# The D term of a selective scan added by a diagonal matrix, its sums read out by ScalarE, and one step-size operation moved from GpSimd to VectorE

## The chip, the core and the metric

The kernel runs on one core of a Trainium2 chip. The metric is the device time of one execution in microseconds, here the median of three runs.

## What is computed

The input x has 8 sequences (batches below) of 1024 steps and 256 channels. A block modulates x, runs a selective scan (Mamba) over each sequence, adds the result, modulates again, and adds a mixture of eight experts, of which each token takes two. Cut to what matters here:

```python
h = _layernorm(x) * (1 + ca) + sa
x_dbl = einsum('bld,ed->ble', h, W_x)              # dt_raw (64), B_sel (16), C_sel (16)
dt = softplus(einsum('blr,dr->bld', dt_raw, W_dt) + b_dt)
A_bar = exp(dt[..., None] * -exp(A_log))
dB_u = (dt * h)[..., None] * B_sel[:, :, None, :]
h_state = scan over l of  A_bar * previous + dB_u
y = einsum('bldn,bln->bld', h_state, C_sel)
x = x + ga * (y + h * D_param)
h2 = _layernorm(x) * (1 + cb) + sb
x = x + gb * mixture_of_experts(h2)
```

The modulation vectors sa, ca, ga, sb, cb, gb come from a small matmul at the start; ga and D_param are inputs, one number for each channel (ga also for each batch).

## The kernel before

**Work and its pieces.** Channels lie on partitions, the 1024 steps along the free dimension. A batch has 32 units: two halves of 128 channels (hf), four groups of states (q), four groups of channels (j). A unit is one tile of 128 partitions (32 channels by 4 states) by 1024. For each unit, ScalarE makes exp(A dt) (`decay`, line 624, into one of three buffers av), VectorE multiplies the spread B in PSUM by dt*u (`times_b`, line 821, the product by B) and scans (`scan`, line 828, into one of eight buffers h), and GpSimd multiplies by C (`times_c`, line 955). For each four units TensorE spreads the next B over the partitions (`spread_b`, line 466, one pair of banks, so it waits for the last product of the four before) and sums the products over the states with a mask that also holds ga (`sums`, line 485, called y). Four such groups make one half of a batch in the banks Y.

**The residual.** When the four groups of a half are summed, VectorE's step zs (line 847) makes ga*D*hT + sums and writes it over hT, in one instruction of 128x1024; TensorE transposes it (`residual`, line 561), and VectorE adds x (zX, line 857).

**The step size.** With v the matmul of dt_raw plus the bias, softplus is relu(v) + log(1 + exp(-|v|)), and for small exp(-|v|) a correction is added: with e = exp(-|v|) and up = 1 + e as rounded, it is log(up) - ((up - 1) - e). ScalarE makes |v|, relu, e, up and the logarithm (lines 658 to 670; tiles sp_t and src), VectorE's step corr makes (up - 1) - e (line 841), and GpSimd's step dt has three operations of 128x512: log minus the correction (line 964), plus relu, which is dt (line 966), and dt times u (line 969). The matmul of dt (line 519), those for B and C (line 514), and the reads of C share one bank. SyncE then copies dt and dt*u, each from 32 partitions to four places, to dd (lines 400 and 407), from which ScalarE and VectorE take them.

**The experts.** GpSimd multiplies h2T by the gates, for two experts at a time (xg, line 987, one of two buffers), TensorE multiplies by the weights (`expert`, line 581: 8 matmuls for each xg, 16 records in the trace, since each fp32 matmul shows as two) and adds the bias (line 589), ScalarE scales (line 704), TensorE transposes (line 550), VectorE adds to x (line 862). There are 16 xg for each batch, and they run beside the units of the next batch. Those of the last batch come behind the last scan.

**What sets the order.** Each engine executes its own list in order. The lists come from one table of times, AT, in units from the start of a batch: `schedule` gives each step a time and sorts, and each engine takes its steps from the sorted list. No step carries out of order, and a wait holds up all that is behind it on its engine. Waits are on counting semaphores: `s_y` counts the groups of sums, `s_z` the residual halves, `s_lp` GpSimd's first step-size operation; `release` and `emptied` are for the shared banks.

```python
            put(s + AT["corr"], "corr", b, hf, c)
            put(s + AT["dt"], "dt", b, hf, c)
...
        put(t + 16 * hf + 16 + AT["zs"], "zs", b, hf)
...
    return [step for _, step in sorted(at, key=lambda p: p[0])]
```

Of the kernel before, what the change touches and what calls it, by code (L numbers as in the profile page):

```python
# [24 lines left out]
AT = dict(exp=0.53, mul=0.02, scan=0.93, ch=8.04, Bs=0.64, y=7.8, stat0=-3.57, stat0s=0.69, rstd0=1.5,  # L25
          rsb0=0.03, xh0=3.5, xh0s=0.29, xT0=15.38, xT0h=0.55, xTs=3.16, rxT0=-0.28, wx=4.64, rwx=-0.1,
          S=-1.08, ldx=34.2, gam=18.44, dl0=20.23, dl1=36.04, dls=3.41, rdl=0.34, corr=0.46, dt=7.7, C=26.08,
          CS=2.58, Cc=1.19, rC=0.34, ddt=37.03, ddts=1.6, ddu=37.35, ddus=2.04, zs=4.0, ldx2=35.93, z=4.84,
          zX=-0.7, zd=2.37, stat1=6.15, stat1s=0.46, rstd1=10.38, rsb1=0.48, xh1=11.48, xh1s=0.0, xh1g=1.96,
          xT1=11.74, xT1h=0.15, xT1s=1.42, rxT1=0.53, lg=13.82, rlg=0.76, lT=0.16, soft=0.58, softe=0.3,  # L30
          top=0.97, gT=1.37, rgT=-0.42, gw=11.16, gr=32.81, xg=23.11, xgs=1.78, gl=-1.9, f=-3.08, fE=0.89,
          o=3.02, oX=1.85, out=11.61, md1=-34.75, gates=-33.15, ga=-25.15, bn0=-118.76, bn0s=9.06,
          stat1A=4.38, stat1B=9.56, stat1sA=4.37, stat1sB=20.83, rstd1A=2.83, rstd1B=8.42, rsb1A=3.19,
          rsb1B=1.49, xh1A=7.29, xh1B=26.22, xh1sA=0.0, xh1sB=0.0, xh1gA=22.13, xh1gB=3.45, xT1A=7.43,
          xT1B=24.5, xT1hA=0.0, xT1hB=1.19, xT1sA=3.31, xT1sB=12.26, rxT1A=2.4, rxT1B=4.65, lgA=9.1,
          lgB=69.91, rlgA=1.11, rlgB=-7.93, lTA=1.32, lTB=5.57, softA=1.74, softB=-9.93, softeA=0.39,
          softeB=4.13, topA=5.19, topB=2.3, gTA=2.65, gTB=16.94, rgTA=-0.31, rgTB=1.96, gwA=20.35, gwB=6.85,
          grA=57.71, grB=94.08, xgA=38.5, xgB=129.13, xgsA=4.99, xgsB=8.34, glA=8.49, glB=20.82, fA=21.21,
          fB=-7.62, fEA=76.63, fEB=43.38, oA=35.72, oB=68.53, oXA=17.7, oXB=61.07, outA=58.55, outB=89.32,
          stat1P=6.67, stat1sP=0.31, rstd1P=9.57, rsb1P=0.13, xh1P=10.69, xh1sP=0.0, xh1gP=2.8, xT1P=12.61,  # L40
          xT1hP=0.0, xT1sP=0.58, rxT1P=0.47, lgP=14.2, rlgP=-0.07, lTP=0.1, softP=0.18, softeP=0.3, topP=0.5,
          gTP=0.86, rgTP=0.23, gwP=10.31, grP=30.17, xgP=22.53, xgsP=1.69, glP=-2.42, fP=-3.58, fEP=0.38,
          oP=4.43, oXP=9.99, outP=34.06)
# [978 lines left out]
```

## Time and profile before

| what | value |
|---|---|
| median of 3 runs | 1219.75 us (1219.33 to 1220.39) |
| the profiled execution, its own time | 1223.0 us |
| its span in the trace | 1221.1 us |
| granted TensorE clock over the span | 0.875 of full |
| VectorE busy | 1024.6 us, 84% |
| GpSimd busy | 1025.0 us, 84% |
| TensorE busy (matmuls) | 943.9 us, 77% |
| ScalarE busy | 712.3 us, 58% |

The profile is of one execution. Its engines are named PE (TensorE), PEld (its weight loads), DVE (VectorE), ACT (ScalarE), POOL (GpSimd) and SP (SyncE, which only issues DMAs; SPq is its queue of instructions). L828 is line 828 of the kernel. A share of busy time is a mean over the whole span, in which the start (the first scan begins at 49.56 us) and the end behind the last scan have other limits than the middle, so stretches and single rows are needed to tell which engine the others wait for.

### The profile page before, as it was taken

What the parts mean: (1) busy time and instruction counts of PE and PEld (TensorE: products, weight loads), DVE (VectorE), ACT (ScalarE), POOL (GpSimd) and SP (SyncE); (2) the same over time, 40 slices, a digit from 0 to 9 for tenths busy, and PEclk for the clock granted to TensorE, in tenths of its full rate; (3) what the DMA queues carried; (4) which work ended last, traced back from release to release, by engine and by line L of the source; (5) the groups of instructions that cost most, each with busy time, mean ns of one, the idle gap of its engine ahead of it and who ended that gap; (6) DMA issues with size and microseconds to landing.
All of it is one profiled execution on the core that took longest, in us unless ns stands there. A gap on an engine that the chain in (4) does not pass through costs nothing. (4 is left out here: it accounts for less than half of the span.)

```text
span 1221.1 us, 13597 instructions
## 1 busy us (share of the span) xinstructions
PE 943.9 (77%) x4235; PEld 591.0 (48%) x4235; DVE 1024.6 (84%) x826; ACT 712.3 (58%) x1412; POOL 1025.0 (84%) x512
## 2 busy tenths in 40 slices
PE   6234543588978888788977888788978986889998
PEld 4101111245644555455554555455644664557787
DVE  2399999999899989999999989999999999995110
ACT  4764578456775579547856678457855366331200
POOL 1477766699999999899999999899989999798453
PEclk9556655589998889899999989999998999889899
DMA  5607060536425371637244551637152533521221
GB/s 163 160 14 181 27 137 1 119 84 171 114 68 146 105 185 44 150 86 193 74 104 106 155 146 46 165 96 183 42 138 81 154 106 94 124 70 52 82 77 61
DMA packets 90552, 131.21 MB, mean 107 GB/s; under 512 B 13536, under 2 KB 73512, under 8 KB 90480
## 3 DMA queue, kind: packets, MB, share of 16 engines
q1 hardware_dynamic: 90480, 130.34, 41.2%
q8 instruction: 34, 0.56, 0.2%
q14 instruction: 38, 0.31, 0.1%
HBM read 54.50 MB, written 8.65 MB: 52 GB/s over the span
## 5 line engine op out<-in xcount | busy, mean ns | idle before, releaser
L955 POOL TENSOR_TENSOR h<-h,Cr 128x1024 f32<-128x1024 f32 x256 | 603.0, 2375 | 64.0 <-DVE h L828 62.2
L828 DVE TENSOR_TENSOR_SCAN h<-av,ps 128x1024 f32<-128x1024 f32 x256 | 584.8, 2284 | 18.0 <-ACT av L624 1.6
L581 PE MATMUL ps<-xg,we 128*128 128x256 f32 x2048 | 495.6, 398 | 30.6 <-POOL xg L987 26.9
L581 PEld LDWEIGHTS ps<-xg,we 128*128 128x128 f32 x2048 | 399.2, 199 | 127.5 <-POOL xg L987 39.5
L987 POOL TENSOR_TENSOR xg<-h2T,gbc 128x1024 f32<-128x1024 f32 x128 | 304.1, 2378 | 62.8 <-DMA gbc<-gates 31.7
L821 DVE TENSOR_TENSOR ps<-ps,dd 128x1024 f32<-128x1024 f32 x256 | 315.4, 1232 | 45.4 <-DMA dd<-src 16.1
L624 ACT ACTIVATE av<-dd,An 128x1024 f32<-128x1024 f32 x256 | 288.2, 1141 | 52.4 <-DVE h L828 40.8
L485 PE MATMUL ps<-h,gam 128*32 128x512 f32 x1024 | 161.7, 761 | 15.4 <-POOL h L955 9.4
L466 PE MATMUL ps<-S,sel 64*128 64x512 f32 x128 | 52.4, 492 | 56.8 <-DVE ps L821 56.5
L704 ACT ACTIVATE z<-ps,md 128x256 f32<-128x256 f32 x64 | 26.7, 468 | 97.9 <-PE ps L589 75.5
L485 PEld LDWEIGHTS ps<-h,gam 128*32 128x32 f32 x1024 | 32.1, 128 | 97.9 <-issue 84.1
L678 ACT ACTIVATE Cr<-ps 128x512 f32<-128x512 f32 x64 | 37.7, 591 | 63.0 <-PE ps L526 42.6
L519 PE MATMUL ps<-rows,wrow 64*128 64x512 f32 x64 | 44.4, 781 | 32.7 <-DVE S L835 24.4
L862 DVE TENSOR_TENSOR X<-ps,X 128x512 f32<-128x512 f32 x32 | 21.9, 684 | 54.3 <-PE ps L550 54.3
L466 PEld LDWEIGHTS ps<-S,sel 64*128 64x128 f32 x128 | 21.7, 210 | 94.4 <-DVE ps L821 80.5
L658 ACT ACTIVATE sp_t<-ps,bd 128x512 f32<-128x512 f32 x32 | 21.8, 683 | 65.9 <-PE ps L519 65.9
L526 PE MATMUL ps<-S,sel 64*128 64x512 f32 x64 | 33.8, 531 | 30.9 <-ACT Cr L678 28.4
L505 PE MATMUL ps<-identf,sp_t 128*128 128x128 f32 x128 | 23.5, 317 | 31.4 <-ACT sp_t L735 20.1
L976 POOL TENSOR_TENSOR gam<-mask,ga 128x256 f32<-128x256 f32 x8 | 5.1, 631 | 48.0 <-DMA ga<-md 27.2
L964 POOL TENSOR_TENSOR src<-src,sp_t 128x512 f32<-128x512 f32 x32 | 41.4, 1294 | 3.5 <-DVE sp_t L841 3.5
L969 POOL TENSOR_TENSOR src<-src,hT 128x512 f32<-128x512 f32 x32 | 40.8, 1274 | 2.5
L966 POOL TENSOR_TENSOR src<-src 128x512 f32<-128x512 f32 x32 | 40.7, 1271 | 2.5
(100 smaller groups left out, 830.6 us busy)
## 6 DMA issues: line engine op xcount, KB each, us to landing
dd<-src SPq DMA_DIRECT2D x512, 128.0 KB, 2.5
gbc<-gates SPq DMA_DIRECT2D x128, 256.0 KB, 3.6
X<-in_x SPq DMA_DIRECT2D x8, 1024.0 KB, 7.3
out<-X SPq DMA_DIRECT2D x32, 256.0 KB, 2.3
XN<-in_x SPq DMA_DIRECT2D x7, 1024.0 KB, 7.1
we<-in_We SPq DMA_DIRECT2D x2, 1024.0 KB, 9.1
XN<-in_x SPq DMA_DIRECT2D x2, 512.0 KB, 4.7
Cr<-in_wmod SPq DMA_DIRECT2D x1, 1024.0 KB, 5.7
```

The source lines that it names most:

```text
L466: e = pe.matmul(ps[:, BQ + c], sel[R:P, q], S[R:P, b % 2, c * CH:(c + 1) * CH], start=True, stop=True)
L485: e = pe.matmul(ps[32 * j:32 * j + 32, Y + c], gam[:, b % 2, 2 * j + hf], h[:, (4 * g + j) % HS, c * CH:(c + 1) * CH], start=(q == 0), sto ...
L519: e = pe.matmul(bk, wdt[:, hf * P:(hf + 1) * P], dtr[:, c * CH:(c + 1) * CH], start=True, stop=True)
L581: e = pe.matmul(bk[:, m * 256:(m + 1) * 256], we[:, hf, 2 * ep + e2, m * P:(m + 1) * P], xg[:, i % XG, e2, hf], start=(ep == e2 == m == hf ...
L624: act.activation(av[:, u % AS], dd[:, j, 0], ACT.Exp, scale=An[:, 0, i:i + 1]).then_inc(s_a, 1)
L821: dve.tensor_tensor(wide(BP), wide(BQ), dd[:, j, 1], ALU.mult).then_inc(s_bm, 1)
L828: dve.tensor_tensor_scan(h[:, u % HS], av[:, u % AS], wide(BP), 0.0, ALU.mult, ALU.add).then_inc(s_scan, 1)
L955: pool.tensor_tensor(h[:, u % HS], h[:, u % HS], Cr[:, q], ALU.mult).then_inc(s_ch, 1)
L964: pool.tensor_tensor(src[:, 1, cs], src[:, 1, cs], sp_t[:, 1], ALU.subtract).then_inc(s_lp, 1)
L966: pool.tensor_tensor(src[:, 0, cs], src[:, 1, cs], src[:, 0, cs], ALU.add).then_inc(s_dt, 1)
L969: pool.tensor_tensor(src[:, 1, cs], src[:, 0, cs], hT[:, b % 2, hf, cs], ALU.mult).then_inc(s_dtu, 1)
L987: pool.tensor_tensor(xg[:, i % XG], h2T[:, :, 256 * c:256 * c + 256].unsqueeze(1).to_broadcast([P, 2, 2, 256]), gbc[:, i % GL].unsqueeze(2 ...
```

## The change

1. VectorE's step zs goes. A diagonal matrix dg (128x128 for each half, the identity scaled by ga*D, made by ScalarE in the new step dg) is multiplied with hT on TensorE, eight matmuls of 32x512 ahead of the first group of sums of each half, in the same accumulation. ScalarE then copies the finished sums from the two banks Y to hT (the new zs).
2. In the step size, VectorE's corr becomes two operations: log + e into the bank, then (up - 1) minus that, over the logarithm in src. GpSimd subtracts the result from relu, which is dt; its step has two operations in place of three. ScalarE's wait for `s_lp` ahead of up becomes a wait for VectorE's release of the bank.
3. The table AT has other numbers.

```diff
+    put(t + AT["dg"], "dg", b)
...
+                if q == 0:
+                    pe.wait_ge(s_dg, b + 1)
                 for c in range(2):
+                    if q == 0:
+                        for j in range(NJ):
+                            pe.matmul(ps[32 * j:32 * j + 32, Y + c], dg[:, hf, 32 * j:32 * j + 32],
+                                      hT[:, b % 2, hf, c * CH:(c + 1) * CH], start=True, stop=False)
                     for j in range(NJ):
                         e = pe.matmul(ps[32 * j:32 * j + 32, Y + c], gam[:, b % 2, 2 * j + hf],
-                                      h[:, (4 * g + j) % HS, c * CH:(c + 1) * CH], start=(q == 0), stop=(q == NQ - 1))
+                                      h[:, (4 * g + j) % HS, c * CH:(c + 1) * CH], start=False, stop=(q == NQ - 1))
...
                     if i:
-                        act.wait_ge(s_lp, i)
+                        emptied(act, ("dl", i // 4 - (i % 4 == 0), (i - 1) % 4 // 2, (i - 1) % 2))
...
+                elif s[0] == "dg":
+                    b = s[1]
+                    if b == 0:
+                        act.wait_ge(s_md, 2)
+                    if b:
+                        act.wait_ge(s_y, 8 * b - 3)
+                    for hf in range(2):
+                        e = act.activation(dg[:, hf], identf[:], ACT.Copy, scale=Dga[:, hf, b:b + 1])
+                    e.then_inc(s_dg, 1)
+                elif s[0] == "zs":
+                    _, b, hf = s
+                    act.wait_ge(s_y, 8 * b + 4 * hf + 4)
+                    act.activation(hT[:, b % 2, hf], wide(Y), ACT.Copy).then_inc(s_z, 1)
...
                     use = ("dl", b, hf, c)
-                    release(dve.scalar_tensor_tensor(out=sp_t[:, 1], in0=sp_t[:, 1], scalar=-1.0, in1=mb(use), op0=ALU.add,
+                    l = src[:, 1, c * CH:(c + 1) * CH]
+                    link(dve.tensor_tensor(mb(use), mb(use), l, ALU.add))
+                    release(dve.scalar_tensor_tensor(out=l, in0=sp_t[:, 1], scalar=-1.0, in1=mb(use), op0=ALU.add,
                                                      op1=ALU.subtract), use)
-                elif s[0] == "zs":
-                    _, b, hf = s
-                    dve.wait_ge(s_y, 8 * b + 4 * hf + 4)
-                    z = hT[:, b % 2, hf]
-                    dve.scalar_tensor_tensor(out=z, in0=z, scalar=Dga[:, hf, b:b + 1], in1=wide(Y), op0=ALU.mult,
-                                             op1=ALU.add).then_inc(s_z, 1)
...
                     emptied(pool, ("dl", b, hf, c))
-                    pool.tensor_tensor(src[:, 1, cs], src[:, 1, cs], sp_t[:, 1], ALU.subtract).then_inc(s_lp, 1)
-                    pool.wait_ge(s_lp, i + 1)
-                    pool.tensor_tensor(src[:, 0, cs], src[:, 1, cs], src[:, 0, cs], ALU.add).then_inc(s_dt, 1)
+                    pool.tensor_tensor(src[:, 0, cs], src[:, 0, cs], src[:, 1, cs], ALU.subtract).then_inc(s_dt, 1)
```

**The order on VectorE, fifth batch, from unit 19 on.** S<-ps,S is the low part of C's rows of the next batch. In the kernel before, L821 is the product by B, L828 the scan, L835 S, L847 zs, L841 corr:

```order
L821 TENSOR_TENSOR ps<-ps,dd 128x1024
L828 SCALAR_TENSOR_TENSOR h<-av,ps 128x1024
L847 SCALAR_TENSOR_TENSOR hT<-hT,Dga,ps 128x1024
L821 TENSOR_TENSOR ps<-ps,dd 128x1024
L841 SCALAR_TENSOR_TENSOR sp_t<-sp_t,ps 128x512
L828 SCALAR_TENSOR_TENSOR h<-av,ps 128x1024
L821 TENSOR_TENSOR ps<-ps,dd 128x1024
L828 SCALAR_TENSOR_TENSOR h<-av,ps 128x1024
L821 TENSOR_TENSOR ps<-ps,dd 128x1024
L835 TENSOR_TENSOR S<-ps,S 32x512
```

The same place in the changed kernel, where L842 is the product, L849 the scan, L856 S, and L863 with L864 corr:

```order
L842 TENSOR_TENSOR ps<-ps,dd 128x1024
L849 SCALAR_TENSOR_TENSOR h<-av,ps 128x1024
L842 TENSOR_TENSOR ps<-ps,dd 128x1024
L863 TENSOR_TENSOR ps<-ps,src 128x512
L864 SCALAR_TENSOR_TENSOR src<-sp_t,ps 128x512
L849 SCALAR_TENSOR_TENSOR h<-av,ps 128x1024
L842 TENSOR_TENSOR ps<-ps,dd 128x1024
L856 TENSOR_TENSOR S<-ps,S 32x512
```

zs is gone, corr has two instructions, and S stands one unit earlier. Elsewhere in a batch corr of the first columns of the second half moves from behind product 4 to behind scan 3 of the next batch's units.

**The order on TensorE at the same place**, from one spread of B to the next. In the kernel before, L581 is an expert group, L514 the matmul for B and C, L519 the matmul of dt, L485 y, L466 the spread of B:

```order
L581 MATMUL ps<-xg,we 128x256 x8
L514 MATMUL ps<-hT,wx 128x512 x2
L581 MATMUL ps<-xg,we 128x256 x8
L519 MATMUL ps<-rows,wrow 128x512
L485 MATMUL ps<-h,gam 32x512 x8
L466 MATMUL ps<-S,sel 128x512 x2
```

In the changed kernel (L490 the diagonal matmuls, L493 y, L468 the spread):

```order
L589 MATMUL ps<-xg,we 128x256 x8
L522 MATMUL ps<-hT,wx 128x512 x2
L589 MATMUL ps<-xg,we 128x256 x8
L527 MATMUL ps<-rows,wrow 128x512
L490 MATMUL ps<-hT,dg 32x512 x4
L493 MATMUL ps<-h,gam 32x512 x4
L490 MATMUL ps<-hT,dg 32x512 x4
L493 MATMUL ps<-h,gam 32x512 x4
L468 MATMUL ps<-S,sel 128x512 x2
```

The list is the same but for the diagonal matmuls, which stand ahead of the spread. The group of y with them has twice the matmuls.

**The end of GpSimd's list**, in the kernel before (L955 the product by C, L987 xg):

```order
L987 TENSOR_TENSOR xg<-h2T,gbc 128x1024
L955 TENSOR_TENSOR h<-h,Cr 128x1024
L987 TENSOR_TENSOR xg<-h2T,gbc 128x1024
L955 TENSOR_TENSOR h<-h,Cr 128x1024 x2
L987 TENSOR_TENSOR xg<-h2T,gbc 128x1024 x22
```

and in the changed one (L972 the product by C, L1002 xg):

```order
L1002 TENSOR_TENSOR xg<-h2T,gbc 128x1024
L972 TENSOR_TENSOR h<-h,Cr 128x1024 x2
L1002 TENSOR_TENSOR xg<-h2T,gbc 128x1024
L972 TENSOR_TENSOR h<-h,Cr 128x1024 x2
L1002 TENSOR_TENSOR xg<-h2T,gbc 128x1024 x23
```

One xg more stands behind the last product by C.

## Rows read from the trace of the kernel before

**Rows 1.** Stretches: length, busy time and instructions of each engine, TensorE's clock, DMA
```profile
core 0: us, PE busy (x) PEld busy (x) DVE busy (x) ACT busy (x) POOL busy (x), PEclk, DMA share, GB/s
69.00:184.00 115.00, 56.10 (x182) 16.40 (x182) 110.64 (x68) 66.06 (x113) 86.74 (x44) 0.63 0.38 92
654.00:772.00 118.00, 100.90 (x464) 65.35 (x463) 110.69 (x80) 80.96 (x171) 113.92 (x56) 0.94 0.42 111
```

**Rows 2.** VectorE in order of time, fifth batch, units 18 to 21 (start us, length us)
```profile
659.22 2.29 DVE L828 TENSOR_TENSOR_SCAN h<-av,ps 128x1024 f32<-128x1024 f32 x1
661.42 1.26 DVE L847 SCALAR_TENSOR_TENSOR hT<-hT,Dga,ps 128x1024 f32<-128x1024 f32 x1
662.59 1.23 DVE L821 TENSOR_TENSOR ps<-ps,dd 128x1024 f32<-128x1024 f32 x1
663.73 0.68 DVE L841 SCALAR_TENSOR_TENSOR sp_t<-sp_t,ps 128x512 f32<-128x512 f32 x1
664.32 2.28 DVE L828 TENSOR_TENSOR_SCAN h<-av,ps 128x1024 f32<-128x1024 f32 x1
666.64 1.23 DVE L821 TENSOR_TENSOR ps<-ps,dd 128x1024 f32<-128x1024 f32 x1
667.96 2.29 DVE L828 TENSOR_TENSOR_SCAN h<-av,ps 128x1024 f32<-128x1024 f32 x1
```

**Rows 3.** Order of time at the start, GpSimd and VectorE
```profile
35.01 1.26 POOL L964 TENSOR_TENSOR src<-src,sp_t 128x512 f32<-128x512 f32 x1
36.35 1.26 POOL L966 TENSOR_TENSOR src<-src 128x512 f32<-128x512 f32 x1
...
40.26 1.27 POOL L966 TENSOR_TENSOR src<-src 128x512 f32<-128x512 f32 x1
...
48.29 1.23 DVE L821 TENSOR_TENSOR ps<-ps,dd 128x1024 f32<-128x1024 f32 x1 [10.11 <-DMA dd<-src]
```

**Rows 4.** Order of time at the end: last scan, last products by C, last experts
```profile
1107.34 2.29 DVE L828 TENSOR_TENSOR_SCAN h<-av,ps 128x1024 f32<-128x1024 f32 x1
...
1109.74 4.71 POOL L955 TENSOR_TENSOR h<-h,Cr 128x1024 f32<-128x1024 f32 x2
...
1200.30 14.08 PE L581 MATMUL ps<-xg,we 128*128 128x256 f32 x64
```

**Rows 5.** Groups by line: busy us, mean ns of one, idle time before and its releasers
```profile
L847 DVE SCALAR_TENSOR_TENSOR hT<-hT,Dga,ps 128x1024 f32<-128x1024 f32 x16 | 20.1, 1257 | 6.3 <-PE ps L485 6.3
L964 POOL TENSOR_TENSOR src<-src,sp_t 128x512 f32<-128x512 f32 x32 | 41.4, 1294 | 3.5 <-DVE sp_t L841 3.5
L485 PE MATMUL ps<-h,gam 128*32 128x512 f32 x1024 | 161.7, 761 | 15.4 <-POOL h L955 9.4
L678 ACT ACTIVATE Cr<-ps 128x512 f32<-128x512 f32 x64 | 37.7, 591 | 63.0 <-PE ps L526 42.6
```

**Rows 6.** VectorE's waits (total, times, longest), then single rows about the waits for spreads
```profile
DVE ps L821 <- PE ps L466: 16.0, 11, 4.2
...
704.10 3.72 PE L581 MATMUL ps<-xg,we 128*128 128x256 f32 x16 [0.28 <-POOL xg L987]
...
709.62 1.23 DVE L821 TENSOR_TENSOR ps<-ps,dd 128x1024 f32<-128x1024 f32 x1 [1.32 <-PE ps L466]
...
718.96 0.69 DVE L862 TENSOR_TENSOR X<-ps,X 128x512 f32<-128x512 f32 x1 [0.68 <-PE ps L550]
...
725.47 1.25 DVE L847 SCALAR_TENSOR_TENSOR hT<-hT,Dga,ps 128x1024 f32<-128x1024 f32 x1
...
726.75 0.59 ACT L670 ACTIVATE src<-ps 128x512 f32<-128x512 f32 x1
...
728.57 1.23 DVE L821 TENSOR_TENSOR ps<-ps,dd 128x1024 f32<-128x1024 f32 x1 [1.85 <-PE ps L466]
...
674.01 2.90 PE L485 MATMUL ps<-h,gam 128*32 128x512 f32 x16
676.84 0.73 PE L466 MATMUL ps<-S,sel 64*128 64x512 f32 x2
678.31 1.23 DVE L821 TENSOR_TENSOR ps<-ps,dd 128x1024 f32<-128x1024 f32 x1
```

More of the change, by code:

```diff
@@ L20 @@
 BP, BQ, Y, FB, MB = 0, 2, 4, 6, 7
[L25 to L43, printed above, removed]
@@ new lines @@
+AT = dict(exp=0.59, mul=0.43, scan=0.96, ch=7.78, Bs=0.44, y=7.6, stat0=-4.54, stat0s=0.89, rstd0=2.74,
+          rsb0=0.6, xh0=4.31, xh0s=0.27, xT0=15.23, xT0h=0.42, xTs=2.79, rxT0=0.56, wx=4.56, rwx=-0.56,
+          S=-0.62, ldx=32.82, gam=24.87, dg=39.13, dl0=20.18, dl1=35.75, dls=3.34, rdl=0.63, corr=0.47,
+          dt=7.55, C=26.12, CS=2.5, Cc=0.92, rC=0.35, ddt=37.04, ddts=2.42, ddu=37.96, ddus=2.38, zs=4.38,
+          ldx2=45.74, z=5.23, zX=-0.54, zd=2.16, stat1=6.33, stat1s=0.53, rstd1=10.61, rsb1=0.09, xh1=10.92,
+          xh1s=0.19, xh1g=1.06, xT1=12.22, xT1h=0.0, xT1s=1.4, rxT1=0.08, lg=13.63, rlg=0.08, lT=0.4,
+          soft=0.94, softe=-0.22, top=1.06, gT=1.34, rgT=0.42, gw=10.17, gr=32.45, xg=23.0, xgs=1.78,
+          gl=-1.86, f=-3.08, fE=1.03, o=2.8, oX=2.34, out=20.48, md1=-19.28, gates=-24.81, ga=-20.38,
+          bn0=-78.02, bn0s=5.5, stat1A=6.02, stat1B=7.93, stat1sA=19.78, stat1sB=30.22, rstd1A=4.66,
+          rstd1B=16.88, rsb1A=4.34, rsb1B=0.0, xh1A=9.01, xh1B=17.46, xh1sA=0.07, xh1sB=2.33, xh1gA=27.4,
+          xh1gB=2.12, xT1A=8.51, xT1B=39.47, xT1hA=0.1, xT1hB=4.62, xT1sA=2.21, xT1sB=15.61, rxT1A=3.27,
+          rxT1B=2.43, lgA=10.46, lgB=76.49, rlgA=2.49, rlgB=-20.32, lTA=1.01, lTB=17.54, softA=1.37,
+          softB=41.67, softeA=1.66, softeB=-10.5, topA=15.02, topB=46.43, gTA=3.65, gTB=39.11, rgTA=1.9,
+          rgTB=9.48, gwA=13.83, gwB=67.25, grA=103.18, grB=175.9, xgA=52.72, xgB=186.07, xgsA=13.74,
+          xgsB=26.38, glA=17.37, glB=11.13, fA=17.19, fB=6.58, fEA=49.37, fEB=28.42, oA=57.91, oB=37.69,
+          oXA=34.38, oXB=63.52, outA=97.14, outB=66.98, stat1P=7.31, stat1sP=0.21, rstd1P=9.63, rsb1P=0.54,
+          xh1P=10.69, xh1sP=0.07, xh1gP=0.82, xT1P=11.33, xT1hP=0.22, xT1sP=0.97, rxT1P=0.14, lgP=12.75,
+          rlgP=1.03, lTP=0.02, softP=0.81, softeP=0.65, topP=0.83, gTP=0.64, rgTP=2.1, gwP=11.81, grP=32.49,
+          xgP=21.34, xgsP=1.95, glP=-4.1, fP=-3.17, fEP=2.41, oP=3.48, oXP=11.77, outP=35.08)
@@ L270, in adaln_block @@
         bns, bna = sb("bns", [P, 4, 6]), sb("bna", [P, BLK, 2])
+        dg = sb("dg", [P, 2, P])
         pe_t, G = sb("pe_t", [P, BLK, E]), sb("G", [P, BLK, E])
@@ L290, in adaln_block @@
         s_dtr, s_hi = sem("s_dtr"), sem("s_hi")
-        s_abs, s_e, s_up, s_l, s_lp = (sem(n) for n in ("s_abs", "s_e", "s_up", "s_l", "s_lp"))
+        s_abs, s_e, s_up, s_l = (sem(n) for n in ("s_abs", "s_e", "s_up", "s_l"))
         s_dt, s_dtu = sem("s_dt"), sem("s_dtu")
```

4 lines of the change are left out of this document (2 added, 2 removed).

## The prediction

> **What bounds the kernel now.** I read the stretches first, then VectorE's instructions in order of time, then what ended its waits, and the chain of waits last. In a stretch of 118 us in the middle [rows 1], VectorE is busy 110.7 us and GpSimd 113.9 us; TensorE has 100.9 and ScalarE 81.0. By share of busy time GpSimd looks like the bound. The order of time says otherwise. VectorE alternates a product by B (line 821) and a scan (line 828): from scan to product 2.32 us, from product to scan 1.32 us [rows 2]. That is 3.64 us for each of 256 units, or 932 us, with 15 residual steps (line 847), 30 corrections (line 841) and smaller steps between, 91 us together. The first product starts at 48.29 us [rows 3], the last scan ends at 1109.63 us [rows 4]: 1061.3 us, so VectorE waits for only 38 us of that stretch. It is the bound, and the others matter by the waits that they cause. Behind the last scan TensorE is the bound: its matmuls of the experts stand almost without a gap until the end, which is also what the chain of waits shows.
>
> **VectorE's own work.** Removed: zs (line 847), 16 times 1.257 us [rows 5], the 16th behind the last scan. What one costs in the stream is read from [rows 2]: scan to zs 2.20, zs to product 1.17, 3.37 in place of 2.32, so 1.05 us, and for 15 of them 15.8 us. Added: a sum of 128x512 ahead of each correction, in PSUM, with a wait between the two. The trace has no such pair of this size. The nearest rows are the correction itself, 0.68 us long, and the step to an instruction that needs the one before it, which costs the length of the first and 0.04 to 0.09 us more (scan to product 2.32 for 2.28, product to scan 1.32 for 1.23) [rows 2]. I take the lower of these, 0.72 us; ends 0.59 (a next instruction that waits for nothing, correction to scan) and 0.77. Two of 32 stand ahead of the first product, so 30 times 0.72 is 21.6 us (17.7 to 23.1). Net **+5.8 us** (+1.9 to +7.3). So the engine that sets the time gets more work, not less.
> The page "VectorE: DVE Perf Modes" of the Trainium skill says in the section "The DRAIN you can't avoid" that a semaphore between two instructions adds nothing, only their count does. By that the pair would cost 0.59 and the net would be +1.9. The row of product and scan speaks against it: 1.32 with the wait, where the correction starts 1.14 behind the product [rows 2].
>
> **Start.** GpSimd gets to the first step-size operation at 35.01 us, and the next starts 1.34 us behind it; SyncE's copies of dt to dd wait for the second half's, at 40.26 + 1.27 us [rows 3]. Two operations fewer stand ahead of that: 2.7 us. ScalarE's wait for the first of them (line 667) becomes a wait for VectorE's correction, which is earlier, so it does not stand in the way. VectorE waits 10.1 us for these copies at 48.29 [rows 3], and its next three products wait for the copies too. The first product can hardly move, since TensorE's first spread of B stands behind reads of C that do not change; the later ones can. **-2.7 us** (0 to -2.7).
>
> **End.** In GpSimd's order one xg more stands behind the last product by C, 23 for 22. So one less is ahead of it: GpSimd finished the last two products by C at 1114.45, 4.8 us behind the last scan [rows 4], where one takes 2.36; the last y can come 2.4 us earlier. TensorE then has one expert group more, 14.08/4 = 3.5 us [rows 4], less some 0.6 us of a gap ahead of the transpose of G that it fills. **+0.5 us** (-2.4 to +3.5). The last zs now runs on ScalarE, under an expert group.
>
> **Where VectorE's waits go.** This term decides. 32 operations of 1294 ns leave GpSimd, 41.4 us [rows 5], but GpSimd isn't the bound, so they count only where VectorE waits for something that was late because of it. GpSimd catches up with the scans once in a batch, near its middle, and is behind through the turn to the next. In the turn three waits stand close together, and they recur in batches 2 to 7: the spread of B at the turn (1.32 us at 709.62), the transposes of the output (0.68 at 718.96), and the spread one group later (1.85 at 728.57) [rows 6]. Eleven waits for a spread make 16.0 us, the longest 4.2 [rows 6]; the one for outputs recurs in most of these batches. Ahead of 709.62 TensorE had waited for xg at 704.10, and the spread stands behind that expert group and the bias [rows 6]. By that turn two subtractions of 1.34 us are gone from GpSimd's queue. 2.7 us cover the wait at the turn whole in five batches (some 6.9 us) and 2.7 of 4.2 in batch 2: 9.6. Of the following two, at most 2.5 us in a batch and, by what the eleven leave, about 7 in sum, I count a third, 2.4, since TensorE is itself late there. Recovered: 12.0 us (0 to 16).
> New waits: TensorE gets 128 matmuls, eight for each of 16 half batches. Those of y take 161.7/64 = 2.53 us for eight on the mean [rows 5] (two records each), so +40 us of TensorE, and each of the 16 y groups doubles. They stand ahead of a spread. At 674.01 y takes 2.90, the spread starts at 676.84 and takes 0.73, VectorE's product starts at 678.31: 0.74 us of slack [rows 6]. The new order answers this: S stands one unit earlier on VectorE, so the matmul of dt ahead of that y can come up to 3.6 us earlier. In the first batch the granted clock is 0.63 of the full one, with TensorE at 1.2 GHz for much of it [rows 1], and this will not suffice: 1.5 us. The first correction of the second half now stands behind scan 3, not product 4: scan 3 ends where zs begins, 725.47, but ScalarE's logarithm ends at 726.75 + 0.59 [rows 6]; 1.8 us in that batch, less in others, in sum 2.5. New waits 4.0 (0 to 15). ScalarE's new zs has half of it priced at 591 ns [rows 5], so at most 1.2 us each, 19 us in sum, in an engine with 37 us idle in 118 [rows 1]; it stands where ScalarE is ahead of the scans by more than that. If that cover is gone, it delays a scan by 1.2 us. Its dg copies are a few tenths. Net **-8.0 us**.
>
> **Sum**: 5.8 - 2.7 + 0.5 - 8.0 = -4.4 us. The profiled execution took 1223.0 us (span 1221.1), 3.25 above the median of 1219.75; it would take 1218.6, and the median comes to **1215.4 us**.
>
> **The rivals.**
> (A) TensorE becomes late: the diagonal matmuls hold up the spread ahead of the seventh group of each batch. For: the slack of 0.74 us [rows 6] against 2.5 us of matmuls on the mean and the 2.90 at that place. Against: S is earlier. It decides where the matmul of dt gains less than those 2 us. Then 2.5 to 2.9 less 0.74, some 2 us in each of 8 batches, 16 us: 3.6 - 12 + 16 = +7.6, **1227.4**, slower. 0.12.
> (B) None of VectorE's waits goes, since the spreads are late by TensorE's own order: 5.8 - 2.7 + 0.5 = +3.6, **1223.4**, slower. Against: the idle time ahead of 704.10 ends with GpSimd. 0.09.
> (C) All of the 16 us go and no new wait comes: **1207.4**. For: GpSimd has 5.2 us less in each batch. 0.12.
> (D) The change takes work off GpSimd but the time does not see it: half of my net recovery, -4 us, against +3.6: -0.4, **1219.4**. 0.20.
> (E) The linked pair costs 0.59 us, not 0.72: my sum with 17.7 for 21.6, **1211.5**. This is what that page's rule comes to. 0.05.
> My forecast has 0.42.
>
> **How the numbers follow.** About 0.2% (2.4 us) is what a measurement of this kernel can tell from no change. Faster: forecast, C and E, 0.59, by 1217.3 or less. Same: D, 0.20. Slower: A and B, 0.21. The range 1209 to 1224 takes in B, D and E and the bounds of the start and the end; it leaves out most of A and the lower part of C.
>
> **What would show it.** Right: VectorE's stream from the first product to the last scan shrinks by 1 to 4 us; a group of 32 sums of some 680 ns on VectorE, with 0.72 to the correction behind; waits for spreads fall from 16 us below 7; GpSimd's busy time falls by some 41 us and the time does not follow it; the first copies to dd start 2.7 us earlier. Wrong: waits for line 466's successor that grow, above all ahead of the seventh group (A); scans that wait for ScalarE behind zs; copies that start no earlier.

## The result and the profile after

The changed kernel took **1232.17 us** (median of 4 runs, 1230.25 to 1233.7), the kernel before 1220.07 us (4 runs beside it, 1219.33 to 1221.18). The ratio is 1.0101, with a 95% interval of 1.0072 to 1.013: **slower by 12.1 us**. The forecast was 1215.4, in a range of 1209 to 1224.

The profiled execution of the changed kernel took 1230.25 us (span 1228.5 us), 1.9 below its median; that of before, 1223.0 us, stands 2.9 above its own. So the two traces differ by 7.3 us, and 4.8 of the 12.1 us are differences from run to run that no trace here shows. TensorE's granted clock doesn't divide the two kernels: 0.874 to 0.880 of full in the four runs of the changed one, 0.875 in the profile of before.

The stretches of [rows 1] in the trace of the changed kernel:

```profile
core 0: us, PE busy (x) PEld busy (x) DVE busy (x) ACT busy (x) POOL busy (x), PEclk, DMA share, GB/s
69.00:184.00 115.00, 59.65 (x213) 17.47 (x212) 109.20 (x68) 64.24 (x111) 78.77 (x39) 0.59 0.37 88
654.00:772.00 118.00, 104.64 (x480) 66.29 (x479) 110.14 (x73) 83.86 (x174) 112.40 (x54) 0.91 0.45 118
```

GpSimd is busy less in both stretches, and TensorE more. ScalarE is busy 2.9 us more in the middle, but 1.8 us less in the first batch. VectorE is busy 1.4 and 0.6 us less, so the stretches alone don't show that its list has become longer or that it waits more. Its new pair, in order of time in the fifth batch (against [rows 2]):

```profile
670.72 0.69 DVE L863 TENSOR_TENSOR ps<-ps,src 128x512 f32<-128x512 f32 x1
671.45 0.69 DVE L864 SCALAR_TENSOR_TENSOR src<-sp_t,ps 128x512 f32<-128x512 f32 x1
672.05 2.28 DVE L849 TENSOR_TENSOR_SCAN h<-av,ps 128x1024 f32<-128x1024 f32 x1
```

From the start of the sum to that of the correction it is 0.73 us here, where the correction needs the sum; from the correction to the scan 0.60. The start and the end (against [rows 3] and [rows 4]):

```profile
34.19 1.27 POOL L981 TENSOR_TENSOR src<-src 128x512 f32<-128x512 f32 x1
...
38.85 1.26 POOL L981 TENSOR_TENSOR src<-src 128x512 f32<-128x512 f32 x1 [2.05 <-DVE src L864]
...
47.16 1.23 DVE L842 TENSOR_TENSOR ps<-ps,dd 128x1024 f32<-128x1024 f32 x1 [8.39 <-PE ps L468]
...
1114.89 2.29 DVE L849 TENSOR_TENSOR_SCAN h<-av,ps 128x1024 f32<-128x1024 f32 x1
```

The first product is 1.1 us earlier, the last scan ends 7.6 us later (1114.89 + 2.29 = 1117.2 for 1109.6), and from there to the end of the span it is 111.3 us for 111.5. So the loss lies between the first product and the last scan. The groups and waits there (against [rows 5] and [rows 6]), first the groups, in busy us, mean ns of one, and idle time before:

```profile
L972 POOL TENSOR_TENSOR h<-h,Cr 128x1024 f32<-128x1024 f32 x256 | 604.5, 2375 | 134.0 <-DVE h L849 134.0
L842 DVE TENSOR_TENSOR ps<-ps,dd 128x1024 f32<-128x1024 f32 x256 | 315.4, 1232 | 45.8 <-DMA dd<-src 17.5 <-PE ps L468 14.9 <-DVE h L849 0.5
L490 PE MATMUL ps<-hT,dg 128*32 128x512 f32 x256 | 40.1, 700 | 16.6 <-DVE X L874 7.3 <-POOL h L972 6.4 <-ACT dg L752 2.9
```

then the waits (total, times, longest):

```profile
DVE ps L842 <- DMA dd<-src: 17.5, 14, 2.4
...
DVE ps L842 <- PE ps L468: 14.9, 6, 8.4
```

GpSimd now waits 134.0 us for scans (62.2 before). VectorE's wait for a spread of B is 14.9 us in sum, but 8.4 of that is the first product, which had waited for a copy before; so those within the stream did shrink from 16.0 to 6.5. In their place it waits 14 times for copies to dd (5 before, the first product's 10.1 us among them). One of the new places, behind unit 18 of the fifth batch:

```profile
663.65 0.70 DVE L856 TENSOR_TENSOR S<-ps,S 32x512 fp32r<-32x512 f32 x1 [0.17 <-ACT S L659]
665.87 1.23 DVE L842 TENSOR_TENSOR ps<-ps,dd 128x1024 f32<-128x1024 f32 x1 [1.52 <-DMA dd<-src]
```

**A ledger for all kernels below.** For each pair of neighbouring instructions on VectorE I took the distance from start to start, and counted as wait what it has above the lower tenth of such pairs in all these traces. The rest is VectorE's own work. How finely the pairs are sorted moves some 3 us between work and waits, all behind unit 14 and in every kernel alike; the differences between kernels stay within 0.6 us. "Behind unit k" (units are counted from 0 to 31 in a batch; unit 31 is the turn to the next batch) sums the waits between product k and product k+1 over the batches. Times in us; the work, waits and end are those of the one profiled execution, the median that of 4 to 12 runs. Before stands between 1218.0 and 1220.1 in the five measurements, and each ratio is to the runs beside it; for two kernels of different measurements the difference by medians and that by ratios lie up to 2.6 us apart.

| kernel | median | own work | waits | unit 31 | 23 | 18 | 14 | 3 | end |
|---|---|---|---|---|---|---|---|---|---|
| before | 1220.1 | 1019.0 | 42.4 | 11.2 | 0.9 | 1.3 | 4.8 | 3.1 | 111.5 |
| changed | 1232.2 | 1024.6 | 45.4 | 6.3 | 0.1 | 12.2 | 4.9 | 0.0 | 111.3 |
| changed, order of before | 1239.3 | 1024.4 | 57.0 | 14.1 | 8.6 | 0.4 | 10.8 | 6.1 | 108.7 |
| before, new order | 1242.1 | 1019.8 | 58.1 | 4.0 | 0.0 | 13.5 | 6.7 | 0.1 | 110.9 |
| D term alone | 1215.8 | 1003.0 | 55.3 | 12.6 | 8.7 | 0.1 | 5.6 | 9.6 | 109.4 |
| D term, no diagonals | 1216.4 | 1003.0 | 51.6 | 9.6 | 0.9 | 0.7 | 11.0 | 6.0 | 110.7 |
| step size alone | 1244.2 | 1040.3 | 46.8 | 14.7 | 2.1 | 0.1 | 11.4 | 0.3 | 108.9 |
| before, GpSimd less | 1215.7 | 1019.0 | 39.5 | 11.2 | 1.5 | 0.1 | 6.7 | 0.0 | 107.2 |
| before, gates moved | 1212.1 | 1019.0 | 34.9 | 5.0 | 0.9 | 0.8 | 7.0 | 3.2 | 109.0 |
| step size, gates moved | 1237.8 | 1040.3 | 38.6 | 1.9 | 4.0 | 0.1 | 11.7 | 2.9 | 109.4 |
| D term, gates moved | 1210.7 | 1003.0 | 47.7 | 1.5 | 6.9 | 0.7 | 13.1 | 3.6 | 108.3 |
| both, order of before, gates moved | 1221.1 | 1024.4 | 35.1 | 0.7 | 6.1 | 0.5 | 8.2 | 3.7 | 110.4 |
| D term, gates moved, S earlier | 1210.5 | 1002.6 | 47.5 | 7.1 | 0.6 | 7.2 | 6.0 | 6.0 | 110.4 |
| changed, SyncE's list of before | 1239.2 | 1024.6 | 53.6 | 10.2 | 0.1 | 5.5 | 8.1 | 2.3 | 111.0 |
| the same, gates moved | 1230.5 | 1024.6 | 37.2 | 1.9 | 0.1 | 5.0 | 8.5 | 0.0 | 111.7 |
| changed, gates' write later | 1231.7 | 1024.6 | 43.4 | 7.8 | 0.2 | 9.2 | 4.9 | 0.1 | 114.2 |
| the same, S later | 1242.5 | 1024.0 | 57.0 | 4.0 | 3.2 | 8.1 | 7.4 | 0.1 | 113.3 |

The waits of the ledger sorted by what ended them, for before and the changed kernel: the spread of B 15.9 and 6.4 us, the transposes ahead of VectorE's additions to x 6.8 and 0.3, copies to dd 5.9 and 17.0, ScalarE's S 0.0 and 6.6, the router's matmul 1.3 and 2.0, ScalarE's logarithm 0.0 and 1.6. So the waits that were there did go, 16.0 us of the first two kinds, and some 19 us came at other places.

### The profile page after: what moved, and what is told of

Same layout as the page of the kernel before. It is cut to its first block and busy times, and to the rows that moved or that the text cites. A ratio compares the mean times of both kernels' runs of the same rounds, so it can differ in the third digit from the quotient of the medians.

```text
span 1228.5 us, 14126 instructions
## 1 busy us (share of the span) xinstructions
PE 966.7 (79%) x4491; PEld 604.7 (49%) x4491; DVE 1028.1 (84%) x842; ACT 732.5 (60%) x1444; POOL 986.4 (80%) x480
## 5 line engine op out<-in xcount | busy, mean ns | idle before, releaser
L972 POOL TENSOR_TENSOR h<-h,Cr 128x1024 f32<-128x1024 f32 x256 | 604.5, 2375 | 134.0 <-DVE h L849 134.0
L849 DVE TENSOR_TENSOR_SCAN h<-av,ps 128x1024 f32<-128x1024 f32 x256 | 584.7, 2284 | 17.8 <-DVE ps L842 0.4
L589 PE MATMUL ps<-xg,we 128*128 128x256 f32 x2048 | 505.2, 404 | 12.7 <-POOL xg L1002 8.0
L589 PEld LDWEIGHTS ps<-xg,we 128*128 128x128 f32 x2048 | 406.2, 203 | 107.2 <-issue 34.5
L842 DVE TENSOR_TENSOR ps<-ps,dd 128x1024 f32<-128x1024 f32 x256 | 315.4, 1232 | 45.8 <-DMA dd<-src 17.5
L1002 POOL TENSOR_TENSOR xg<-h2T,gbc 128x1024 f32<-128x1024 f32 x128 | 304.0, 2376 | 61.7 <-PE ps L589 27.7
L493 PE MATMUL ps<-h,gam 128*32 128x512 f32 x1024 | 149.2, 694 | 13.2 <-POOL h L972 13.2
L468 PE MATMUL ps<-S,sel 64*128 64x512 f32 x128 | 52.8, 496 | 74.7 <-DVE ps L842 74.5
L468 PEld LDWEIGHTS ps<-S,sel 64*128 64x128 f32 x128 | 21.4, 208 | 109.2 <-DVE ps L842 97.5
L493 PEld LDWEIGHTS ps<-h,gam 128*32 128x32 f32 x1024 | 32.1, 122 | 87.2 <-issue 70.2
L527 PE MATMUL ps<-rows,wrow 64*128 64x512 f32 x64 | 39.8, 704 | 23.9 <-DVE S L856 8.6
L490 PE MATMUL ps<-hT,dg 128*32 128x512 f32 x256 | 40.1, 700 | 16.6 <-DVE X L874 7.3
L513 PE MATMUL ps<-identf,XN 128*128 128x128 f32 x128 | 27.7, 358 | 29.0 <-DVE X L879 17.7
L648 ACT ACTIVATE h2T<-ps,md 128x512 f32<-128x512 f32 x32 | 24.7, 777 | 37.8 <-PE ps L513 34.5
L656 ACT ACTIVATE rows<-ps 64x512 f32<-64x512 f32 x16 | 9.4, 591 | 57.5 <-PE ps L522 57.5
## 6 DMA issues: line engine op xcount, KB each, us to landing
X<-in_x SPq DMA_DIRECT2D x8, 1024.0 KB, 7.3
XN<-in_x SPq DMA_DIRECT2D x7, 1024.0 KB, 6.1
we<-in_We SPq DMA_DIRECT2D x2, 1024.0 KB, 8.2
Cr<-in_wmod SPq DMA_DIRECT2D x1, 1024.0 KB, 4.9
```

The source lines that it names most:

```text
L468: e = pe.matmul(ps[:, BQ + c], sel[R:P, q], S[R:P, b % 2, c * CH:(c + 1) * CH], start=True, stop=True)
L490: pe.matmul(ps[32 * j:32 * j + 32, Y + c], dg[:, hf, 32 * j:32 * j + 32], hT[:, b % 2, hf, c * CH:(c + 1) * CH], start=True, stop=False)
L527: e = pe.matmul(bk, wdt[:, hf * P:(hf + 1) * P], dtr[:, c * CH:(c + 1) * CH], start=True, stop=True)
L589: e = pe.matmul(bk[:, m * 256:(m + 1) * 256], we[:, hf, 2 * ep + e2, m * P:(m + 1) * P], xg[:, i % XG, e2, hf], start=(ep == e2 == m == hf ...
L842: dve.tensor_tensor(wide(BP), wide(BQ), dd[:, j, 1], ALU.mult).then_inc(s_bm, 1)
L849: dve.tensor_tensor_scan(h[:, u % HS], av[:, u % AS], wide(BP), 0.0, ALU.mult, ALU.add).then_inc(s_scan, 1)
```

## The experiments

**The four corners and the two parts.** "Order of before" is the table AT of before with two additions that the new steps need:

```diff
-zs=4.0, rstd1A=2.83, rsb1A=3.19
+zs=4.38, rstd1A=4.66, rsb1A=2.0, dg=39.13
```

Changed arithmetic in that order:

> The changed arithmetic in the order of before (the numbers of AT of before, the new step dg at 39.13, zs on ScalarE at 4.38, and two numbers of ScalarE's list moved so that zs of the last half comes ahead of rstd). SyncE's list is that of before. Theory Q (the loss is the new order of SyncE's queue, which starts the copies to dd later ahead of the product that needs them): 1213 to 1220 us, and VectorE's waits on DMA are those of the start alone (some 16 us). Theory P (TensorE's diagonal matmuls make spreads of B late): 1227 to 1233 us, with waits of the product by B on TensorE above 16 us. Theory W (VectorE's +7 us of its own work, nothing else matters): 1225 to 1227 us.

Measured 1239.26 us, ratio to before 1.0167 (1.0145 to 1.0189). The arithmetic of before in the new order, its table AT swapped in whole:

> The arithmetic of before in the order of the changed kernel (its numbers of AT, without dg). Theory Q: slower than before by 5 to 12 us (1225 to 1232), with waits of the product by B on the copies to dd of more than 20 us in sum. Theories P and W: within 3 us of before (1217 to 1223), since neither a diagonal nor a second operation of corr is there.

Measured 1242.12, ratio 1.0193 (1.0169 to 1.0218). The D term alone (the diff without its part 2, in the order of before with the two additions):

> Only the D term is changed (diagonal matmuls on TensorE, zs on ScalarE); the step size has its three operations on GpSimd and one on VectorE; order of before. VectorE has 15 x 1.05 = 15.8 us less work ahead of the last scan. Theory Q or W: 1204 to 1212 us, faster than before. Theory P: the gain is lost to later spreads, 1218 to 1228 us, with waits of the product by B on TensorE of 25 us or more.

Measured 1215.77, ratio 0.9972 (0.9952 to 0.9993). The step size alone (part 2 without the D term, in the order of before):

> Only the step size is changed (two operations on VectorE, two on GpSimd); zs stays on VectorE; order of before. VectorE has 30 x 0.71 = 21 us more work, the start is 1 us earlier, and some of its waits go. Theory Q: 1228 to 1236 us. Theory P: the same range, since no diagonal is there. Theory W: 1239 to 1242 us, all of the work and no wait recovered. If this and the D term alone sum to the changed kernel in the order of before, the two parts don't act on each other.

Measured 1244.17, ratio 1.0199 (1.0174 to 1.0224).

What follows: theory Q fell with the first, since with SyncE's list of before the changed arithmetic is slower, not faster (its waits for copies to dd fell to 3.8 us, and those for the spread are 39.0, 29.2 of them after the first product; that speaks for P, though the time is 6 us above P's range). The second, 10 us above the range of Q, has 37.1 us of waits for copies to dd, as Q says. I take its copies to be late because GpSimd has a third operation ahead of them; no run tests that. Each order suits the arithmetic it goes with: before loses 22 us in the new one, the changed arithmetic 7 in the old one. The ledger shows the two parts: the D term takes 16.0 us of work off VectorE and gives 12.9 back as waits; the step size adds 21.3 us of work, and no wait of VectorE goes for it in sum (46.8 for 42.4), though it takes 41 us off GpSimd; it came out 2 us above what theory W (all of the work, no wait recovered) says. That was the part on which the forecast rested.

**What holds VectorE at the turn of the batches.** In the step size alone, GpSimd, then SyncE's queue (SPq), TensorE and VectorE at one turn:

```profile
852.57 2.35 POOL L988 TENSOR_TENSOR xg<-h2T,gbc 128x1024 f32<-128x1024 f32 x1 [4.54 <-DMA gbc<-gates]
...
845.79 2.41 SPq L408 DMA_DIRECT2D dd<-src  x4
848.30 0.53 SPq L442 DMA_DIRECT2D gbc<-gates  x1
...
854.98 5.40 PE L582 MATMUL ps<-xg,we 128*128 128x256 f32 x16 [1.81 <-POOL xg L988]
...
844.49 1.23 DVE L822 TENSOR_TENSOR ps<-ps,dd 128x1024 f32<-128x1024 f32 x1
...
862.20 1.23 DVE L822 TENSOR_TENSOR ps<-ps,dd 128x1024 f32<-128x1024 f32 x1 [3.17 <-PE ps L467]
```

GpSimd stands idle for 4.54 us. It waits for the gates of its next xg, whose copy stands in SyncE's list behind the four copies of dt*u for the next batch's first product, and those wait until VectorE has made product 28 (it ends at 844.49 + 1.23 = 845.72, and they are issued at 845.79). Then come xg, TensorE's experts, and the spread of B behind them (line 467). It is a ring through VectorE itself, and a lighter GpSimd only waits longer in it. That is theory G. The trace of the kernel before has the same ring, at 709.62 of [rows 6] and at the other turns:

```profile
695.07 2.40 SPq L407 DMA_DIRECT2D dd<-src  x4
697.57 0.53 SPq L441 DMA_DIRECT2D gbc<-gates  x1
...
701.65 2.39 POOL L987 TENSOR_TENSOR xg<-h2T,gbc 128x1024 f32<-128x1024 f32 x1 [0.23 <-DMA gbc<-gates]
...
300.13 2.36 POOL L987 TENSOR_TENSOR xg<-h2T,gbc 128x1024 f32<-128x1024 f32 x1 [2.61 <-DMA gbc<-gates]
435.29 2.36 POOL L987 TENSOR_TENSOR xg<-h2T,gbc 128x1024 f32<-128x1024 f32 x1 [2.31 <-DMA gbc<-gates]
970.90 2.35 POOL L987 TENSOR_TENSOR xg<-h2T,gbc 128x1024 f32<-128x1024 f32 x1 [2.40 <-DMA gbc<-gates]
```

At five of these six turns, into the third to the eighth batch, GpSimd waits for the copy, 2.61, 2.31, 0.23, 1.06 and 2.40 us. The one that the prediction reads, 0.23, is the shortest of them: GpSimd was there ahead of the copy already.

The rival of G is R: the waits stand where the arithmetic and the other engines' lists put them, and SyncE's list only shows them. G was tried with GpSimd alone made lighter (the kernel before, less its line 964, so that dt lacks the correction; ScalarE's wait for `s_lp` becomes one for VectorE's release of the bank, as in the change):

```diff
-pool.tensor_tensor(src[:, 1, cs], src[:, 1, cs], sp_t[:, 1], ALU.subtract).then_inc(s_lp, 1)
-pool.wait_ge(s_lp, i + 1)
```

> The kernel before with GpSimd's first step-size operation left out (log minus the correction; the correction is made and not used, so dt lacks it), nothing added to VectorE, same order. It takes the 41 us off GpSimd alone. My prediction's step on VectorE's waits says -12 us or so and the start -2.7: about 1205 to 1209. Theory G (GpSimd is held at the turn of the batches by the copy of the gates for its next xg, which stands in SyncE's list behind copies that wait for VectorE's products; a GpSimd with less work only waits longer there): 1216 to 1221 us, and GpSimd's waits for that copy grow from 31.7 us to over 45.

Measured 1215.70, ratio 0.9978 (0.9949 to 1.0006). GpSimd at the turn of 709.62 in [rows 6], where it had waited 0.23 us for that copy, and then its wait over the run (total, times, longest):

```profile
700.60 2.39 POOL L985 TENSOR_TENSOR xg<-h2T,gbc 128x1024 f32<-128x1024 f32 x1 [3.23 <-DMA gbc<-gates]
```

```profile
POOL xg L985 <- DMA gbc<-gates: 44.4, 14, 9.8
```

GpSimd has 41 us less to do and waits 12.7 us longer for the gates. Behind unit 31 VectorE waits 11.2 us, the same as before. All its waits together shrink by 2.9 us, where 12 were forecast; the time, just below G's range, is 3.2 us less than before's, and its interval takes in no change. At each of the six turns GpSimd now waits 3.2 to 4.7 us for the copy. Then the copy was moved, one place at each of the six turns and nothing else in SyncE's list (gl in AT from -1.9 to -1.7, and gw, which must stay ahead, from 11.16 to 10.9):

```diff
+L442 DMA gbc<-gates 128x2x256
 L408 DMA dd<-src 32x1024 x4
-L442 DMA gbc<-gates 128x2x256
```

> As the step-size part alone (1244.2 us), with one move in SyncE's list: the copies of the gates stand 0.2 units earlier, so that at the turn one is ahead of the copies of dt*u for the first product. Theory G: VectorE's waits at the turn (14.6 us behind unit 31 in the run without the move) fall below 6, and the time by 6 to 12 us, to 1232 to 1238. Theory R: no change, 1242 to 1246.

Measured 1237.81, ratio 1.0153 (1.0131 to 1.0174), 6.4 us less. The same turn:

```profile
842.00 0.53 SPq L442 DMA_DIRECT2D gbc<-gates  x1
842.62 2.41 SPq L408 DMA_DIRECT2D dd<-src  x4
...
846.36 2.37 POOL L988 TENSOR_TENSOR xg<-h2T,gbc 128x1024 f32<-128x1024 f32 x1 [1.56 <-DMA gbc<-gates]
...
849.88 3.72 PE L582 MATMUL ps<-xg,we 128*128 128x256 f32 x16
...
855.95 1.23 DVE L822 TENSOR_TENSOR ps<-ps,dd 128x1024 f32<-128x1024 f32 x1
```

TensorE and VectorE wait for nothing here. Behind unit 31 the waits went from 14.7 to 1.9 us. The same move with the D term alone, in the kernel before, and with both parts in the order of before:

> As the D term alone (1215.8 us), with the same move of the copies of the gates in SyncE's list. Theory G: the waits behind unit 31 (12.5 us) fall by half or more, 1206 to 1212 us, faster than before by over 0.5%. Theory P (TensorE is late there by its own work, the diagonals included): 1213 to 1218 us.

> The kernel before with only the gates' copies earlier in SyncE's list. Theory G: in before the gates' copy and GpSimd's own load reach the turn within 0.3 us of each other, so the move alone gains little, 1215 to 1219 us. Rival: SyncE's list was the whole reason of the 11 us at the turn, 1208 to 1212, and the D term adds nothing to the version that beats both.

> The changed arithmetic in the order of before (1239.3 us) with the copies of the gates 0.2 units earlier in SyncE's list, as in the two runs with that move. Theory G: VectorE's waits behind unit 31 (14 us) fall to a few, the time by 5 to 8 us, to 1231 to 1235: as far as the changed kernel's own table came (1232). VectorE's own work stays 5 us above before, so it stays slower than before. Against it, if the move only helps a kernel with one of the two parts: 1237 to 1241.

Measured 1210.68 (ratio 0.9941, 0.992 to 0.9962), 1212.10 (0.9954, 0.9937 to 0.9971) and 1221.08 (1.0031, 1.0013 to 1.0048). The move takes 5 us off the D term, as expected, and 6 off before (1212.1 for the 1218.0 measured beside it), more than I expected, since I had taken GpSimd's load and the copy to be level at the turns from the 0.23 us of one of them; and 18 us off both parts together (17 by the ratios), where 5 to 8 were expected. That is the strongest result for G. It also shows what the changed order is worth: it has the same copy ahead in its list, and still is 11 us slower (9 by the ratios) than both parts in the order of before with the move alone.

**Are the diagonals to blame?** In the D term alone, TensorE and then VectorE:

```profile
670.70 1.12 PE L528 MATMUL ps<-rows,wrow 64*128 64x512 f32 x2 [2.40 <-DVE S L857]
671.75 1.56 PE L491 MATMUL ps<-hT,dg 128*32 128x512 f32 x8
...
677.02 0.73 PE L469 MATMUL ps<-S,sel 64*128 64x512 f32 x2
...
677.78 1.23 DVE L843 TENSOR_TENSOR ps<-ps,dd 128x1024 f32<-128x1024 f32 x1 [1.18 <-PE ps L469]
```

This is rival A, word for word: ahead of the seventh group the diagonals come between the matmul of dt, which waits for S, and the spread, and product 24 waits 1.2 us. Two runs tried it, one without the diagonals (y lacks D times h), and one with S a unit earlier (S in AT from -1.08 to -1.7, the gates moved too):

```diff
-pe.matmul(ps[32 * j:32 * j + 32, Y + c], dg[:, hf, 32 * j:32 * j + 32],
-          hT[:, b % 2, hf, c * CH:(c + 1) * CH], start=True, stop=False)
```

> The D term alone (1215.8 us), but without the diagonal matmuls on TensorE: y lacks D times h, and 128 matmuls of 32x512 are left out; zs is still read out by ScalarE. Theory P (the 13 us of new waits in the run with the D term are TensorE's, by these matmuls, above all the spreads ahead of products 24 and 4): waits of the product by B on the spread fall from 32.7 to about 16 us, the time to 1203 to 1208. Rival: the waits come from the missing zs itself (VectorE reaches what is bound to SyncE or GpSimd sooner), then 1213 to 1217.

> The D term alone with the gates' copies earlier (1210.7 us), and S of the second columns one unit earlier on VectorE (behind product 21, not 22), so that TensorE's matmul of dt, which waits 2.4 us for it, comes ahead of the diagonals sooner. Theory P: the waits ahead of product 24 (6.9 us over the batches) go, 1204 to 1208 us. Rival: something else in the gates' chain is late next (the waits at unit 14 for the router's matmul grow), 1209 to 1212.

Measured 1216.39 (ratio 0.9989, 0.997 to 1.0009) and 1210.53 (0.9952, 0.9928 to 0.9976). In both the wait behind unit 23 went, from 8.7 to 0.9 us and from 6.9 to 0.6, and the time stayed where it was (1215.8 and 1210.7). The waits came back elsewhere: without the diagonals behind unit 14 (5.6 to 11.0, for the router's matmul), with S earlier behind unit 18 (0.7 to 7.2; S now waits for ScalarE) and 31 (1.5 to 7.1). So what theory P says of the place is right, and what it says of the time is not: the wait behind unit 23 can go without a gain. The run without the diagonals has less weight than it seems, since TensorE's busy time fell by 10.8 us only, 958.0 to 947.2, with 40.9 us of matmuls left out. Its experts took 21 us longer, first with the diagonals and then without:

```profile
L590 PE MATMUL ps<-xg,we 128*128 128x256 f32 x2048 | 480.9, 390 | 33.5 <-POOL xg L1003 29.3
L586 PE MATMUL ps<-xg,we 128*128 128x256 f32 x2048 | 502.3, 402 | 29.1 <-POOL xg L999 22.6
```

The granted clock was 0.889 with them and 0.870 without (the medians of twelve runs each are 0.892 and 0.872). What the diagonals would cost at the same clock no run shows. What is late next, once VectorE has less to do, is not one engine: in these traces the waits behind units 14, 18, 23 and 31 take each other's place.

**What the new order costs.** SyncE's list of before in the changed kernel (its times gw, gl, out, ldx2, ddt, ddu and their like from AT of before, nothing else; the order of its last two batches has numbers of its own in AT and stays in part the new one):

> The changed kernel, but SyncE takes its steps in the order of before (the times of its own steps in AT from before); all other engines keep the changed order. Theory Q (what is left of it after the first four runs: the waits behind S at unit 18 and at unit 2, 7.6 + 5.2 us, are for copies to dd that this queue issues late): 1219 to 1225 us, with waits of the product by B on these copies down to the start's. Against it, theory R (the changed kernel's waits stand where the arithmetic and the other engines' lists put them, and SyncE's list only shows them): within 3 us of the changed kernel, 1229 to 1235 us.

Measured 1239.20, ratio 1.0177 (1.0161 to 1.0193): slower still, and outside what either theory said. Behind unit 18 the waits fell from 12.2 to 5.5 us, and rose behind unit 31 from 6.3 to 10.2, behind 14 from 4.9 to 8.1. The copies to dd were late by SyncE's list (17.0 us in the stream of the changed kernel, 4.5 here), which is the half of Q that held. The time did not follow: waits for the spread rose from 6.4 to 13.3, for the router's matmul from 2.0 to 5.8, for ScalarE's logarithm from 1.6 to 5.9. Beside the other engines' new lists the new list of SyncE is the better one. With the gates moved as well, and, in the changed kernel as it is, first gw alone from 10.17 to 11.1, then S from -0.62 to 0.0 too:

> The changed kernel with SyncE's list of before and the copies of the gates 0.2 units earlier, that is the run with SyncE's order of before (1239.2 us) plus the move that took 18 us off in the order of before (1239.3 to 1221.1). If SyncE's list is what divides these kernels: 1220 to 1226 us, below the changed kernel. If the lists of the other engines matter as much: 1228 to 1236.

> The changed kernel with one step moved in SyncE's list: the write of the gates stands behind the copies of dt*u for the second product of the second half, not ahead of them. Its waits behind unit 18 (12.2 us over the batches, 7.6 of them for these copies) are then gone to the greater part if that write is what makes the copies late: 1224 to 1229 us. If they are late for another reason: 1230 to 1234.

> As the run with the later write of the gates, and VectorE's two S steps of a batch one unit later (behind units 19 and 22, as in before the second was), since the first waits for ScalarE (4.4 us behind unit 18, 2.2 behind unit 21). If both waits are local: 4 us below that run, 1220 to 1225. If VectorE then only meets the next late thing (the spread ahead of product 24, which waits for S by way of the matmul of dt and the diagonals): no gain against it.

Measured 1230.52 (ratio 1.0086, 1.006 to 1.0111), 1231.72 (1.0095, 1.0059 to 1.0131) and 1242.50 (1.0194, 1.0156 to 1.0231). The move of the gates takes 8.7 us off SyncE's order of before here as well (11 by the ratios), but the runs of that kernel lie between 1222.7 and 1236, and its profile is of the fastest, so its row of the ledger reads too low. The write of the gates was not the cause of the loss: with it later the waits for copies to dd go from 17.5 to 10.4 us and the time does not follow. S later is worse by 11 us, where a gain or nothing was expected: the waits behind unit 2 go from 6.0 to 10.9 and behind unit 20 from 3.2 to 8.5. **Still open** is which of the other engines' lists makes the remaining 9 to 11 us between the changed kernel and both parts in the order of before.

## Why the prediction was wrong

**What bounds the kernel** held, as far as it went: VectorE's stream from the first product to the last scan sets the time, and GpSimd's share of 84% did not make it the bound: 41 us less on it gave 3.2.

**VectorE's own work**: +5.8 forecast, +5.6 in the ledger (1024.6 for 1019.0). zs was worth 16.0, the 30 sums 21.3. The linked pair costs 0.71 us from start to start by the lower quartile of 32 and 0.72 by the median, the 0.72 of the forecast; from the correction to the scan, which needs nothing of it, 0.60. With that rival E falls. The Trainium skill's rule ("VectorE: DVE Perf Modes", "The DRAIN you can't avoid", that a semaphore between two instructions adds nothing, measured there on eight copies) is not what this trace shows for a dependent pair of 128x512: 0.11 us more each, 3.3 us over 30.

**Start**: -2.7 forecast, -1.1 measured; the second half's subtraction now waits 2.05 us for VectorE's correction, which the forecast had not counted. The copies to dd start 1.4 us earlier (40.14 for 41.56), not 2.7, and by the fourth product that is the gain (62.26 for 63.64). **End**: +0.5 forecast, -0.2 measured.

**Where VectorE's waits go** is the step that failed: -8.0 forecast (12.0 recovered, 4.0 new), +3.0 measured. By the sorting above, the waits for spreads and transposes that the prediction named shrank by 16.0, and some 19 us came at other places. Two terms of it:
- "By that turn two subtractions of 1.34 us are gone from GpSimd's queue. 2.7 us cover the wait at the turn." GpSimd's last wait ahead of that turn was 0.23 us for the copy of the gates, and I read it as a GpSimd without slack. In fact the copy set the time of that xg, here and at four other turns, where GpSimd waited up to 2.6 us for it. 41 us less on GpSimd recovered 2.9 us; the copy one place earlier recovered 7.5. The changed kernel's 4.9 us less behind unit 31 go with that copy's place, which its table holds and of which the prediction says nothing: with SyncE's list of before 3.9 of them come back. So the sign that the prediction gave, waits for spreads below 7 us, came true (6.5) by another cause than the one it stands for; that is luck.
- "New waits 4.0 (0 to 15)." This term was off by the most: some 19 us came, above the upper bound, 11.1 of them for copies to dd and 6.6 for S. I looked for them on TensorE and for the logarithm. 10.9 us came behind unit 18, for copies to dd and for ScalarE's S, in lists that I had compared at the turn and at one place on TensorE alone. SyncE's list I did not compare at all.

**The median**: I took the profile of before to stand 3.25 us above a firm median, from three runs within 1.1 us. In later measurements runs of the same kernel lay between 1211.5 and 1226.1. Over these 82 runs time and granted clock go together (the fastest had 0.888 of full, the slowest 0.868; correlation -0.73); which of the two follows from the other is not shown. The terms of the traces come to -1.1 + 5.6 + 3.0 - 0.2 = +7.3, the medians to +12.1.

**The rivals.** A named a real place, but in the order of before only: behind unit 23 the changed kernel waits 0.1 us. Its time, 1227.4, was the nearest, by chance. B (no wait goes, 1223.4) was right about GpSimd; its reason was wrong, for the move of the copy in SyncE's list alone took 6.2 of the 11.2 us at the turn away (5.0 left). None of them had the changed kernel's own order as the thing that costs. C was never near. D halved a recovery of which the greater part was not there.

The version that beats both is the D term alone in the order of before with the gates' copies moved: 1210.7 us, and 1210.5 with S earlier. But the move alone makes 1212.1, so the D term's own share, 1.4 us, is too small to be told from nothing.

## What to carry to other kernels

An engine that is busy 84% and "waits 0.23 us" for a copy at the place that counts is not shown to be the late one: read that wait at every turn, not at one, and look at when the copy was issued, what stands ahead of it in the queue that issues it, and what that waits for. Where a change brings a new table for a list scheduler, compare every list, the DMA queue's first, and if there is only one experiment, run the new arithmetic in the old order. Work taken off an engine is worth its full length only while nothing else stands within that length behind it: here 16 us of VectorE's work bought 3.6 us.

The Trainium skill, "DMA: Bandwidth & Descriptors", section "Rules for kernel authors", asks to issue a DMA early and wait late. The traces agree: one place earlier in SyncE's list, ahead of four copies that take 2.4 us to issue and of what they wait for, was worth 5 to 18 us.
